# Attention with four PSUM banks for the scores and three for the maxima instead of three and four

## The reference

```
qkv = (h @ Wqkv + bqkv).reshape(B, L, 3, H, HD)
q, k, v = jnp.moveaxis(qkv, 2, 0)
scale = HD ** (-0.5)
attn = jnp.einsum('blhd,bmhd->bhlm', q, k) * scale
attn = jax.nn.softmax(attn, axis=-1)
out = jnp.einsum('bhlm,bmhd->blhd', attn, v).reshape(B, L, D)
return out @ Wproj + bproj
```

## Time and profile before

| | us |
|---|---|
| median of 3 runs | 3332.46 |
| lowest and highest | 3331.38, 3334.86 |
| profiled execution | 3338.19 |
| its span | 3336.4 |

### The profile page before, as it was taken

The page is one execution under the profiler, slowest core; times in us unless marked ns, Lnnn a source line. Parts: engine busy times, 40 slices in busy tenths (PEclk is TensorE's granted clock), DMA queues, the critical chain, the costliest instruction groups (busy, mean ns, idle before and its releaser), DMA issues. The chain is left out here.

```text
span 3336.4 us, 44756 instructions
## 1 busy us (share of the span) xinstructions
PE 3197.1 (96%) x16788; PEld 2173.0 (65%) x16788; DVE 1948.2 (58%) x3352; ACT 1568.2 (47%) x2879; POOL 1617.1 (48%) x800
## 2 busy tenths in 40 slices
PE   7899989998999999999999999999979799999998
PEld 5788877775555555555555555555437688888887
DVE  1477764445887787787877877877526322222222
ACT  0122224431566666666666666666635432222221
POOL 2366520000587787787887877887864100000000
PEclk9999989997899999999999999999989899999999
DMA  5233324445487667686676786676558421111100
GB/s 195 61 126 98 123 74 169 170 154 154 110 193 171 153 163 175 155 200 162 153 171 167 163 197 159 151 175 165 126 158 288 151 89 41 42 41 41 41 19 13
DMA packets 198863, 446.89 MB, mean 134 GB/s; under 512 B 65871, under 2 KB 87631, under 8 KB 167942
## 3 DMA queue, kind: packets, MB, share of 16 engines
q1 hardware_dynamic: 140006, 250.23, 22.1%
q0 software_dynamic: 18432, 134.23, 20.3%
q10 hardware_dynamic: 40224, 59.78, 7.6%
HBM read 157.39 MB, written 84.44 MB: 72 GB/s over the span
## 5 line engine op out<-in xcount | busy, mean ns | idle before, releaser
L1314 DVE TENSOR_REDUCE att_mx<-att_pM 128x1 f32<-128x512 f32 x2048 | 1252.5, 679 | 330.4 <-PE att_pM L1372 329.0
L1299 ACT ACTIVATE att_prob<-att_pS 128x512 f32<-128x512 f32 x2048 | 1047.6, 620 | 402.1 <-PE att_pS L1419 398.9
L1232 POOL TENSOR_TENSOR att_acc<-att_acc,att_prob 128x2048 f32<-128x2048 f32 x224 | 1032.3, 4608 | 208.4 <-ACT att_prob L1299 197.3
L1419 PE MATMUL att_pS<-att_qs,att_ks 98*128 98x512 f32 x2048 | 848.8, 416 | 2.4 <-ACT att_prob L1299 2.1
L1372 PE MATMUL att_pM<-att_ks,att_qs 96*128 96x512 f32 x2048 | 833.5, 415 | 13.0 <-DMA att_ks<-qk_d 12.8
L1419 PEld LDWEIGHTS att_pS<-att_qs,att_ks 98*128 98x128 f32 x2048 | 385.5, 189 | 361.2 <-issue 203.0
L1387 PE MATMUL att_pO<-att_prob,att_V 128*32 128x512 f32 x4096 | 495.7, 602 | 0.0
L1372 PEld LDWEIGHTS att_pM<-att_ks,att_qs 96*128 96x128 f32 x2048 | 398.8, 195 | 103.9 <-DVE att_mx L1314 40.6
L1959 PE MATMUL mlp_pu<-mlp_hs,mlp_W 128*128 128x512 f32 x1536 | 370.5, 390 | 14.2 <-POOL mlp_hs L1902 14.2
L1959 PEld LDWEIGHTS mlp_pu<-mlp_hs,mlp_W 128*128 128x128 f32 x1536 | 289.4, 189 | 74.9 <-POOL mlp_hs L1902 14.6
L1889 ACT ACTIVATE mlp_tu<-mlp_pu,keep_cols 128x512 f32<-128x512 f32 x128 | 88.2, 689 | 504.2 <-PE mlp_pu L1959 504.2
(11 more groups left out here) (229 smaller groups left out, 3020.4 us busy)
## 6 DMA issues: line engine op xcount, KB each, us to landing
att_gathered<-att_prob POOLq DMA_DIRECT2D x128, 1024.0 KB, 8.2
att_gathered<-att_prob SPq DMA_DIRECT2D x64, 1024.0 KB, 6.3
qk_d<-graph_LW SPq DMA_DIRECT2D x64, 512.0 KB, 2.8
att_qs<-qk_d ACTq DMA_DIRECT2D x42, 512.0 KB, 7.1
att_ks<-qk_d ACTq DMA_DIRECT2D x42, 512.0 KB, 10.3
gat_xT<-in_xT SPq DMA_DIRECT2D x32, 256.0 KB, 3.3
gat_xrow<-in_x SPq DMA_DIRECT2D x32, 256.0 KB, 3.0
x_d<-gat_xrow SPq DMA_DIRECT2D x32, 256.0 KB, 2.0
```

The source lines that it names most:

```text
L1232: nc.gpsimd.tensor_tensor(acc[half][:], old[:], new[:], ALU.add).then_inc(added, 1)
L1299: nc.scalar.activation(prob[step % PR][:, c, :], pS[at % 3][:], ACT.Exp, scale=SCALE).then_inc(exp_done, 1)
L1314: nc.vector.tensor_reduce(mx[:, q // 4, q % 4:q % 4 + 1], bank(at)[:], AX.X, ALU.max).then_inc(m_read, 1)
L1419: nc.tensor.matmul(pS[at % 3][:], ks[k][:, h, mt * P:(mt + 1) * P], qs[k][:, h, (2 * half + c % 2) * 512:(2 * half + c % 2 + 1) * 512], st ...
```

## The change

One bank goes from `pM` to `pS`. The bank of a score is now its turn modulo 4 and its wait is for the exponential four turns back; the bank of a maxima tile is its place modulo 3 and its wait is for the reduction three places back. No instruction is added, removed or moved on any engine: the lists of instructions of both kernels are the same for each engine but for the values that the waits of TensorE name. The whole diff:

```
-        pS = [m.ps(f"pS{i}") for i in range(3)]
-        pM = [m.ps(f"pM{i}") for i in range(4)]
+        pS = [m.ps(f"pS{i}") for i in range(4)]
+        pM = [m.ps(f"pM{i}") for i in range(3)]

         def bank(at):
-            return pM[at % 4]
+            return pM[at % 3]

         def wait_bank(pe, at):
-            if at >= 4:
-                pe.wait_ge(m_read, at - 3)
+            if at >= 3:
+                pe.wait_ge(m_read, at - 2)

# scalar engine, copy_sums
-                nc.scalar.activation(zs[:], pS[at % 3][:], ACT.Identity).then_inc(exp_done, 1)
+                nc.scalar.activation(zs[:], pS[at % 4][:], ACT.Identity).then_inc(exp_done, 1)

# scalar engine, the exponentials
-                        nc.scalar.activation(prob[step % PR][:, c, :], pS[at % 3][:], ACT.Exp, scale=SCALE).then_inc(exp_done, 1)
+                        nc.scalar.activation(prob[step % PR][:, c, :], pS[at % 4][:], ACT.Exp, scale=SCALE).then_inc(exp_done, 1)

# tensor engine, finish (all four sums likewise from pS[at % 3] to pS[at % 4])
-                pe.wait_ge(exp_done, at - 2)
+                pe.wait_ge(exp_done, at - 3)

# tensor engine, scores (its matmul likewise from pS[at % 3] to pS[at % 4])
-                if at >= 3:
-                    pe.wait_ge(exp_done, at - 2)
+                if at >= 4:
+                    pe.wait_ge(exp_done, at - 3)
```

More of the change, by code:

```diff
@@ L1403, in finish @@
                 at = turns_of[n]
-                pe.wait_ge(exp_done, at - 2)
-                sums(pS[at % 3], prob[(n % 2 * MT + LAST) % PR], True, False)
+                pe.wait_ge(exp_done, at - 3)
+                sums(pS[at % 4], prob[(n % 2 * MT + LAST) % PR], True, False)
                 for i in range(2):
                     pe.wait_ge(sent[i], (n + 1) * 32)
-                    sums(pS[at % 3], gathered[i], False, False)
+                    sums(pS[at % 4], gathered[i], False, False)
                 pe.wait_ge(added, (n + 1) * NA)
-                sums(pS[at % 3], acc[n % 2], False, True).then_inc(s_done, 1)
+                sums(pS[at % 4], acc[n % 2], False, True).then_inc(s_done, 1)
             def scores(g, step, c):
@@ L1416, in scores @@
                 k, h = g % U, c // 2
-                if at >= 3:
-                    pe.wait_ge(exp_done, at - 2)
-                nc.tensor.matmul(pS[at % 3][:], ks[k][:, h, mt * P:(mt + 1) * P], qs[k][:, h, (2 * half + c % 2) * 512:(2 * half + c % 2 + 1) * 512],
+                if at >= 4:
+                    pe.wait_ge(exp_done, at - 3)
+                nc.tensor.matmul(pS[at % 4][:], ks[k][:, h, mt * P:(mt + 1) * P], qs[k][:, h, (2 * half + c % 2) * 512:(2 * half + c % 2 + 1) * 512],
                                  start=True, stop=True).then_inc(s_done, 1)
```

## The result

| | before | after |
|---|---|---|
| median of 6 runs, us | 3334.56 | 3422.93 |
| lowest and highest | 3331.38, 3337.59 | 3419.83, 3427.95 |
| profiled execution, span | 3336.4 | 3426.1 |

The ratio is 1.0263, with a 95% interval from 1.0253 to 1.0274: the change costs 88 us. The forecast was 3425 us, and 93 us by its sum.

What follows compares the result with a forecast made beforehand. The attention was taken as bound by TensorE. Regular bursts 72.2, transpose bursts 17.7 and transfer bursts 3.4 sum to 93.3 us, taking the median from 3332.46 to 3425.8, stated as 3425; range 3399 to 3447, 82 in 100.

Steps and rivals of the forecast that it cites:

- The wait of tile 7 and its price: Regular bursts: maxima tile 7 waits for reduction 4, so the values start 0.39 us later; 185 bursts, 72.2 us.
- The low and the high bound: Price of the maxima's wait: 66.5 us if the weight load costs nothing, 120 if tile 6's uncovered load is paid too.
- Bursts with a transpose: Bursts where a transpose uses a place among the maxima: values 0.59 us later, 30 bursts, 17.7 us.
- the counts of bursts: Attention: 243 full bursts of maxima, of them 185 regular, 30 with a transpose and 28 with transfers.
- Bursts with transfers: Bursts where ACT issues loads between exponentials: values only 0.12 us later because they already stall; 28 bursts, 3.4 us.
- The last cycles without maxima ... only move.: End of the attention, and the phases behind: claimed to shift in time only, with no gain or loss.
- The rival on the clock: Attention cycles: new waits for DVE bring PE's low clock now and then; one cycle in ten gives 3546 us; 5 in 100.
- PE's granted clock is 1.00 all through the attention: Attention in the kernel before: PE's granted clock taken as 1.00 throughout, against 0.50 in the stretch of maxima alone.
- The stretch of maxima alone: zero: Stretch paced by DVE at 0.60 us a tile: three banks fit with 0.27 us to spare, so no cost.
- The first burst: First burst, at half clock: matmuls 0.43 us apart, a tile each 0.86, slower than DVE, so zero cost.

Runs made afterwards that it cites:

- the late bank: Kernel before with moved transfers, plus one maxima bank as fourth score bank from step 13 of the last unit: 3323.13 us, ratio 0.9968 to the kernel before.

## Why the prediction was right

- **The wait of tile 7 and its price (0.39 us a regular burst).** Right in place and size. The 185 regular bursts lost 0.395 us each. The release took 0.05 to 0.06 us and the way from the load to the values 0.42 to 0.44, which the bursts with a transpose had shown before. Faster reductions took the loss away, and so, but for 10 us, did shorter bursts; the maxima's half alone gave all of it.
- **The low and the high bound.** Neither: 93.8 us in the bursts, against 66.5 and 120 for the whole. By the Trainium skill's rule ("TensorE: Matmul & The Clock Gate", Part 1) that weight loads are pulled ahead, it would have been the low one. The new rows agree with the old: a load whose bank is not free yet is not pulled past its wait, and the matmul behind it starts uncovered.
- **Bursts with a transpose (0.59) and the counts of bursts.** Right: +17.7 us over 30.
- **Bursts with transfers (0.12).** Right: 0.10 us each, their own stall was swallowed, and the fourth score bank gained nothing there. Moving the transfers in the kernel before showed that the stall was real, 7.9 us.
- **"The last cycles without maxima ... only move."** This step failed. I had seen that ScalarE needs 0.48 us an exponential but looked at the scores only beside maxima, where they come 0.47 apart. Without maxima they come 0.23 apart, and then the number of score banks decides: 5.43 us a cycle with three, 4.93 with four. Up to the last sums 8.6 us came from there, 5.2 by the shorter cycles and an estimated 3.4 by the clock, and 5.0 went back to GpSimd's additions and the transfers behind them at the very end, 3.7 net. It is most of the distance between the 93.3 of the sum and the 88.4 measured; the rest, about a microsecond, is within the spread of the runs. The step also took the clock there for granted. In the seven profiles with three score banks and long bursts it was at 0.50 for 7 to 17 us of the end, up to the last sums; in the four with a fourth score bank there, never (nor with three and short bursts). So how much the fourth bank brings at the end differs between executions.
- **The rival on the clock.** Did not happen where it was feared: 1.00 through the whole part with maxima, 0.50 in the stretch of maxima alone as before. "PE's granted clock is 1.00 all through the attention" was wrong for the end of the kernel before, where it fell to 0.50 and rose again while the scores waited for their three banks, and the change took this away. What the Trainium skill tells in "TensorE: Matmul & The Clock Gate", "A second HAM failure mode: psum-queue depth-cycling", agrees with this end. It does not hold for the bursts with maxima, where the loads of the last tiles wait up to 0.30 us each and the clock stayed at 1.00. In the stretch of maxima alone with halved reductions there was one steady level for each number of banks and no going up and down.
- **The stretch of maxima alone: zero.** Right but for 0.6 us, which is small and regular: from the first maxima to the first score it is 53.3 us in three profiles of three with three maxima banks and whole reductions, 52.7 in five of five with four, and 52.1 in the one with five. Each bank lets PE run one reduction of 0.60 us further ahead. The first burst was zero as said (9.5 and 9.6 us), though only its first 12 of 22 matmuls come 0.43 apart.

## What to carry to other kernels

The number of banks that a stream needs is set by the lag of its reader within a burst, not by its mean load: VectorE was busy 79% of the attention and idle at the end of each cycle, and still one bank fewer cost 0.39 us each time. Take the timeline of one burst, write down when each reader's record ends, and check each matmul against the one that frees its bank; where the trace shows such a wait anywhere, its price is there too. A busy share of 100% on a pipelined engine hides waits shorter than the overlap of its records: compare the count of instructions in a stretch, or the idle time of the weight loads. And look at the end of a stage by itself: the balance of the engines is another there, and here both the score banks and the clock counted at the end alone.

## What the runs showed of the hardware

With a matmul's weight load uncovered, what follows starts 0.11 us later than with a covered one (0.43 against 0.32 us). In a stretch of maxima matmuls alone, each read by a VectorE reduction that takes 0.33 us, three banks went with a granted clock of 0.50 and 0.43 us a tile (three profiles of three), four banks with 1.00 and 0.33 us (two of two). In cycles of eight scores that wait for ScalarE and sixteen matmuls of values, with three score banks, the clock was at 0.50 for 7 to 17 us out of 71 to 76 (seven of seven profiles); with four it stayed at 1.00 for all 62 or 63 us (four of four). That the banks cause it is supported by two pairs of kernels that differ in the score banks alone there (three and three against four and three; the moved transfers without and with the late bank); by which mechanism is not shown.
